# Loading the context already turned, instead of turning it on the chip

## What is computed

```python
def _L0_xattn_ref(key, value, query):
    sim = jnp.einsum('ncs,nds->ncd', key, query) * KC ** (-0.5)   # KC = 128 tokens
    sim = jax.nn.softmax(sim, axis=1)
    context = jnp.einsum('ncd,nds->ncs', sim, value)
    return context
...
x = x + _L0_attn_ref(_layernorm(x, axis=-1), L0_attn_w_q, L0_attn_w_k, L0_attn_w_v, L0_attn_w_o)
x = x + _L0_xattn_ref(ctx_4096, ctx_4096, _layernorm(x, axis=-1))
x = x + _L0_ffn_ref(_layernorm(x, axis=-1), ...)
```

## Time and profile before

| | |
|---|---|
| median of 3 runs | 766.47 us (765.67 to 766.51) |
| the profiled execution | 766.96 us, its span 764.9 us |
| TensorE busy | 740.2 us (97%) |
| VectorE, ScalarE, GpSimd busy | 508.7, 387.0, 309.0 us |
| granted TensorE clock, mean | 0.995 of full |
| moved by DMA | 54.34 MB |

### The profile page before, as it was taken

One profiled execution on the slowest core, in us unless ns is written; L12 is line 12 of the kernel. 1 busy time (PEld: TensorE's weight loads), 2 busy tenths in 40 slices (PEclk: granted clock), 3 DMA queues, 4 the chain that ended last, 5 costly groups with the idle time before them and its releaser, 6 DMA issues.

```text
span 764.9 us, 11284 instructions
## 1 busy us (share of the span) xinstructions
PE 740.2 (97%) x3764; PEld 619.2 (81%) x3764; DVE 508.7 (67%) x669; ACT 387.0 (51%) x969; POOL 309.0 (40%) x334
## 2 busy tenths in 40 slices
PE   7999999999999999999999999999999969999994
PEld 6888888888888888888888888888888747888873
DVE  6457736864675577457836864675447877998897
ACT  3365536443553555265536443553566655656642
POOL 4352314322331432152314322331334543689886
PEclk9999999999999999999999999999999999999998
DMA  9412033212313040213023101303500002212102
GB/s 298 117 57 79 1 106 110 78 41 65 131 57 96 10 168 9 96 57 111 0 86 110 58 33 34 132 5 123 165 1 2 1 0 56 69 55 77 28 10 110
DMA packets 43807, 54.34 MB, mean 71 GB/s; under 512 B 7400, under 2 KB 26024, under 8 KB 43784
## 3 DMA queue, kind: packets, MB, share of 16 engines
q1 hardware_dynamic: 43784, 54.05, 21.9%
HBM read 43.16 MB, written 10.88 MB: 71 GB/s over the span
## 4 chain that ended last, share of the span: by engine, by line
PE 89%; DVE 4%; issue 2%; POOL 2%; ACT 1%; DMA 1%; POOLq 0%; SPq 0%; DVEq 0%; ACTq 0%
PE psum L439 20%; PE psum L441 20%; PE psum L440 20%; PE psum L566 7%; PE psum L628 5%; PE psum L629 5%; PE psum L575 3%; PE psum L650 2%; PE psum L651 2%; PE psum L445 1%; DVE stats L1096 1%; PE psum L459 1%; DMA xacc<-in_x 1%; DVE xacc L1212 1%; PE psum L544 0%
## 5 line engine op out<-in xcount | busy, mean ns | idle before, releaser
L1012 POOL TENSOR_TENSOR probs<-probs,rowinv 128x512 f32<-128x512 f32 x64 | 71.2, 1112 | 308.5 <-DVE rowinv L1241 308.5
L830 ACT ACTIVATE probs<-probs,negmax 128x128 f32<-128x128 f32 x256 | 99.8, 391 | 60.3 <-DVE negmax L1228 60.3
L439 PE MATMUL psum<-xt_hi,wq_hi 128*128 128x512 f32 x256 | 104.4, 408 | 0.0
L439 PE MATMUL psum<-wo_hi,at_hi 128*128 128x512 f32 x256 | 100.2, 391 | 0.5 <-DVE at_lo L1259 0.5
L823 ACT CAST pt_hi<-psum 128x512 fp32r<-128x512 f32 x64 | 37.6, 587 | 124.6 <-PE psum L575 124.6
L441 PE MATMUL psum<-xt_hi,wq_lo 128*128 128x512 f32 x256 | 100.2, 391 | 0.0
L440 PE MATMUL psum<-xt_lo,wq_hi 128*128 128x512 f32 x256 | 99.9, 390 | 0.0
L441 PE MATMUL psum<-wo_hi,at_lo 128*128 128x512 f32 x256 | 99.7, 389 | 0.0
L440 PE MATMUL psum<-wo_lo,at_hi 128*128 128x512 f32 x256 | 99.6, 389 | 0.0
L1259 DVE TENSOR_TENSOR at_lo<-psum,at_hi 128x512 fp32r<-128x512 f32 x64 | 44.1, 689 | 72.8 <-ACT at_hi L859 72.8
L734 ACT ACTIVATE qt<-psum 128x512 f32<-128x512 f32 x64 | 38.1, 595 | 75.7 <-PE psum L441 74.1
(11 more groups left out here) (136 smaller groups left out, 1641.6 us busy)
## 6 DMA issues: line engine op xcount, KB each, us to landing
wq_raw<-in_L_attn_w_q SPq DMA_DIRECT2D x8, 1024.0 KB, 5.4
wo_raw<-in_L_attn_w_o SPq DMA_DIRECT2D x8, 1024.0 KB, 7.7
unpacked_w<-u_q SPq DMA_DIRECT2D x8, 688.0 KB, 3.0
gw<-unpacked_w SPq DMA_DIRECT2D x20, 256.0 KB, 3.5
unpacked_w<-u_q SPq DMA_DIRECT2D x6, 512.0 KB, 2.6
u_q<-in_L_ffn_gate_qweight SPq DMA_DIRECT2D x8, 344.0 KB, 7.3
u_q<-in_L_ffn_up_qweight SPq DMA_DIRECT2D x8, 344.0 KB, 3.8
u_q<-in_L_ffn_down_qweight SPq DMA_DIRECT2D x10, 256.0 KB, 3.3
```

The costliest lines, as they stand in the source:

```text
L439: pe.matmul(dst, a_hi, b_hi, start=start, stop=False)
L830: e = act.activation(probs[:, t % 2, j, :], probs[:, t % 2, j, :], ACT.Exp, bias=negmax[:, t % 2, j:j + 1], accum_out=rowsum[:, t % 2, j:j ...
L1012: pool.tensor_tensor(probs[:, t % 2], probs[:, t % 2], rowinv[:, t % 2, :].unsqueeze(2).to_broadcast([P, HG, P]), ALU.mult).then_inc(prob_ ...
```

## The change

The kernel gets the context a second time as `ctx_turned`, a [512, 1024] array: the same numbers, width first, laid out by the host. SyncE loads it straight into `cxt`, in two halves of 1 MB. The first goes over `wq_raw` and waits until all first-half weights of the last pass are split (`w_lo`). The second goes over the k and v weights and waits until the v projection of the last pass is done. Both stand between the load of `cx` and the first loads of `gw`. `turn_context` on TensorE (32 transposes), `context_first` on ScalarE (8 copies) and their two semaphores are gone. `cross_scores` waits for the two loads, `cross_output` for the load of `cx`; what had waited for the copies to release PSUM bank 5 waits for `proj_out`.

```diff
-    CTX_FILL = {t: (2 * (t - 2), 2 * (t - 2) + 1) for t in range(2, 2 + NB // 2)}
...
+            cxt_v = ctx_turned.rearrange("(c p) t -> p c t", p=P)
+            sp.wait_ge(w_lo, LAST * UNITS + FIRST_UNITS)
+            sp.dma_start(cxt[:, 2:HC], cxt_v[:, 2:HC]).then_inc(ld_cxt, 16)
+            sp.wait_ge(proj_done, LAST * NBLK + FIRST_BLOCKS + BLOCKS.index(("v", 1)) + 1)
+            sp.dma_start(cxt[:, 0:2], cxt_v[:, 0:2]).then_inc(ld_cxt, 16)
...
-            def turn_context(t, k):
-
-                if t in CTX_FILL:
-                    b = CTX_FILL[t][k]
-                    if b == 0:
-                        pe.wait_ge(ld_cx, 16)
-                    elif CTX_BANK[b] == CTX_BANK[b - 1]:
-                        pe.wait_ge(cx_out, b)
-                    else:
-                        pe.wait_ge(proj_out, CTX_BLOCKS)
-                    turn_tile(CTX_BANK[b], cx[:, b, :]).then_inc(cx_turned, 1)
...
-                    pe.wait_ge(cx_out, max(b + 1, CTX_BANK.index(BK_FT)))
+                    pe.wait_ge(ld_cxt, 16 * 2)
...
                     pe.wait_ge(xs_prob, b + 1)
+                    pe.wait_ge(ld_cx, 16)
...
-                        pe.wait_ge(cx_out, NB)
+                        pe.wait_ge(proj_out, CTX_BLOCKS)
...
-                    if not more:
-                        turn_context(t, 0)
...
-                        turn_context(t, 1)
...
-            def context_first(t, k):
-
-                if t in CTX_FILL:
-                    b = CTX_FILL[t][k]
-                    act.wait_ge(cx_turned, b + 1)
-                    act.copy(cxt[:, :, b * P:(b + 1) * P],
-                             psum[:, CTX_BANK[b], :].rearrange("p (c t) -> p c t", c=HC)).then_inc(cx_out, 1)
...
+        if name == "ctx_turned":
+            a = np.asarray(inputs["ctx_4096"])
+            a = a.reshape(-1, a.shape[-1]).T
```

More of the change, by code:

```diff
@@ L23, with decoder_kernel @@
 PRIME = 2
-def decoder_kernel(nc, x, ctx_in, w_q, w_k, w_v, w_o,
+def decoder_kernel(nc, x, ctx_in, ctx_turned, w_q, w_k, w_v, w_o,
                    gate_q, gate_s, gate_z, up_q, up_s, up_z, down_q, down_s, down_z, out):
@@ L124, in decoder_kernel @@
         BK_XT, BK_XS, BK_XC, BK_FT = BK_VT, 7, 3, 5
-        CTX_BANK = [BK_XS] * 4 + [BK_FT] * 4
         unpacked_w = nc.dram_tensor("unpacked_w", [STRIPS, P, INTER], F32)
@@ L182, in decoder_kernel @@
         ld_cx = sem("ld_cx")
+        ld_cxt = sem("ld_cxt")
         consts_pool = sem("consts_pool")
@@ L218, in decoder_kernel @@
         o_added = sem("o_added")
-        cx_turned = sem("cx_turned")
-        cx_out = sem("cx_out")
         xs_done = sem("xs_done")
@@ L838, in group @@
                         v_first(n)
-                    if not more:
-                        context_first(t, 0)
                     for i in FILL[t]:
@@ L865, in group @@
                         queries_out(t)
-                        context_first(t, 1)
                     for unit in SPLIT.get(t, ()):
@@ L1365, in columns @@
     return a.reshape(rows, -1, P).transpose(2, 1, 0)
-_INS = ["x", "ctx_4096", "L0_attn_w_q", "L0_attn_w_k", "L0_attn_w_v", "L0_attn_w_o",
+_INS = ["x", "ctx_4096", "ctx_turned", "L0_attn_w_q", "L0_attn_w_k", "L0_attn_w_v", "L0_attn_w_o",
         "L0_ffn_gate_qweight", "L0_ffn_gate_scales", "L0_ffn_gate_zeros",
@@ L1380 @@
     for name in _INS:
-        a = inputs[name]
+        if name == "ctx_turned":
+            a = np.asarray(inputs["ctx_4096"])
+            a = a.reshape(-1, a.shape[-1]).T
+        else:
+            a = inputs[name]
         if name.endswith("_scales"):
```

## The result

Over 20 runs of each kernel, the changed kernel takes 765.70 us (median, 763.18 to 769.51) and the kernel before 768.48 (765.67 to 770.61). The ratio is 0.9969 [0.9956, 0.9981]: 0.31% faster, or about 2.4 us, with 1.5 to 3.4 us in the interval. A second set of runs, made with the experiments, gives 0.9965 [0.995, 0.998]. The forecast was a gain of 2.20 us, 0.29%. The size of the gain fits the forecast, but the twenty runs leave it open whether it exceeds the 0.2% from which the forecast speaks of faster: the interval begins at 0.19%. The level was not as forecast. The three runs of before that were shown are three of the four lowest among the twenty, and 764.3 was too low by 1.4 us.

A forecast was written before the change was run, and what follows sets the result against it. TensorE was taken as the bound where it runs back to back, other engines' chains elsewhere. Five turns at 0.44 us sum to 2.20 us, taking the 766.47 us median to 764.3 us; range 762.8 to 765.8.

The forecast's parts named there:

- rival 3: A second low-clock stretch of the same size behind 630, giving 765.8 us; chance 0.12.
- (a): TensorE, last pass: one tile's turn is four matmuls and costs 0.44 us; all eight would be 3.5 us.
- (b): Slot t = 2: turns of tiles 0 and 1 are links; everything behind moves by 0.88 us.
- (c): Slot t = 3: tile 2's turn is off the chain, before TensorE's wait for `xn`; worth 0.
- (d): Tiles 3, 4 and 5 are links; the shift reaches 2.20 us at the attention scores of t = 5.
- (e): Tiles 6 and 7: TensorE's further lead is lost because VectorE is the later input at t = 6's mask.
- (g): From t = 6 up to 630.75, every link moves by 2.20 us.
- the low stretch: TensorE at the lower clock from 630.75 to 633.87, price 1.5 us; going away or moving gives 762.8 us, chance 0.08.
- (h): SyncE's loads of `cxt` (9.4 us taken) and the queued `gw` arrive in time; worth 0.
- (f): VectorE's scaling of `xprobs` can't finish while GpSimd multiplies; shift stays 2.20 us, removed ScalarE copies worth 0.
- rivals 4 and 5: 4: waits eat tiles 3 to 5, gain 0.88 us, chance 0.07. 5: lower clock 614 to 630, 769.3 us, 0.04.
- Rival 1: Scaling not held by GpSimd (2.67 us), or VectorE not the later input in t = 6 (3.08); chance 0.12.

The follow-up runs named there:

- the repeat: The changed kernel, unchanged, run and profiled once more: 764.22 us.
- the timed profile: Profile from timing the unchanged changed kernel again beside the kernel before: median 765.33 us, ratio 0.9965.
- experiment 4: Changed kernel with the exponential of the cross scores written to PSUM, where VectorE's scaling of `xprobs` reads it: 763.24 us.
- turns alone: Changed kernel with all eight turns put back on TensorE, results unread, no ScalarE copies: 771.08 us.
- copies alone: Changed kernel with eight spare ScalarE copies put back, no turns: 63.31 us from the last pass's first mask to its last `pt_lo`.
- exponential in PSUM with copies: Changed kernel with the cross-score exponential in PSUM, plus eight spare ScalarE copies: 767.02 us.
- the timed exponential in PSUM: Changed kernel with the cross-score exponential in PSUM, timed beside the kernel before: median 765.10 us, ratio 0.9961.

## Where the prediction failed, and where it held

**The step that failed is the last of the sum: the base.** "The median becomes 764.3" sets the gain of 2.20 on 766.47, the median of three runs. Twenty runs of before have the median 768.48, 2.0 us above it; three runs that agree to 0.8 us were taken for the kernel's level, and the spread of twenty is 5 us. With the right base the same sum gives 766.3, and 765.70 was measured. That 765.70 lies inside the range at all, by 0.1 us, is luck: the upper end, 765.8, was made for a second low stretch (rival 3), not for a base 2 us too low. The step behind it has the same fault. It takes 0.2% (1.5 us) for what a measurement can tell from no change, and gives 0.73 to a gain beyond that. The measured gain is 0.31% with an interval from 0.19% to 0.44%, so a gain is clear and one of more than 0.2% is not. Which of the unsteady terms below lifts the median by 2 us stays open, since the runs without a profile don't show them.

**Each step, by what was measured.** (a) and (b): 0.88 us for tiles 0 and 1, at 0.44 a turn, were forecast; putting them back costs 0.85 to 0.88. (c): tile 2 is worth nothing; the wait for `xn` became 0.81 (0.8 to 0.9 forecast), and 0.40 with tile 2 back. (d): the scores of t = 5 at 574.03 for a forecast 574.0. (e): the mask of t = 6 came without a wait at 583.51 - 0.32 = 583.19 (583.2 forecast), and tiles 6 and 7 are worth nothing. TensorE's scores of t = 6 were forecast near 581 and came at 581.32, since TensorE waits in t = 5 for the bank of the cross output, which VectorE's addition behind the scaling sets free: the wait for VectorE that the prediction announced. (g): 2.17 and 2.19 us reach the end of M. The first gate matmul behind the last wait was forecast at 628.5 or 628.6; it came at 628.34 in the repeat and at 628.36 + 0.22 = 628.58 in the timed profile, but at 629.67 in the first one, where the low stretch moved in front of it. (h): the second load of `cxt` lands 4.9 us after its issue, where 9.4 was taken, and nobody waits.

**(f) was right in what it said and too short in what it covered.** The scalings of slots 4 and 5 take 0.84 and end 0.08 behind GpSimd, as forecast, and experiment 4 shows the hold by taking it away. But "the removed ScalarE copies are therefore worth 0" was looked at in slot 5 alone. In slot 4 a copy stands before `xn`, and once the turns are gone it costs 0.2 us. The sum didn't suffer, since (d) had already moved everything up to 576.19 by all five turns, which is right only with the copies gone. (d) called `query_t` of tile 0 the nearest input that TensorE must find, with 0.5 us to spare. Nearer was `xn` of slot 4, and the rows of before could tell it. It ends at 574.07 and, as part of t = 4, moves by the three turns ahead of that slot's scores, to 572.75. TensorE comes for it at 574.46 less four turns, 572.70. So with the copies in place `xn` would be the later one. Without them it comes half a microsecond sooner: in the changed kernel it ends at 572.62 and TensorE is ready for it at 573.06.

**The unsteady terms were half seen.** The prediction named the low stretch and its price, 1.5 us. The profiles show it moved from 630 to 614 (first profile of the changed kernel), absent until 740 (both profiles of the exponential in PSUM) and doubled (turns alone, copies alone). Moving cost 1.08 us in one piece and gave 1.28 in the next. In the changed kernel it stands at 614 in one profile and behind 626 in two, so there its place belongs to the execution and not to the program; for the other kernels this isn't shown. The first profile of the changed kernel alone shows the signs that the prediction gives for rivals 4 and 5: a gate matmul near 629.9 and a granted clock under 1.00 before 628. Neither rival happened. M is 2.17 shorter in that same profile, where rival 4 has 0.88, and the clock's loss in cross comes back in turn-over. Rival 1 didn't happen either: the scaling takes 0.84 us in slots 4 and 5. What the prediction didn't have are two more unsteady terms, each of the same size: the feed-forward's pace (1.55 us) and a low stretch behind the last addition (0.5 to 1.75 us). Whether transposes hold the clock up the way matmuls do, these runs can't tell: it is 1.00 from 551 to 585 with the turns and without.

A reader of the two first profiles alone would have found equal spans and looked for a loss in the feed-forward that isn't the change's. The repeats of both kernels removed that question.

## What to carry to other kernels

Work taken off a busy engine is worth its slots only up to the next place where another engine's result comes later: here five turns of eight, told in advance by which waits stood behind each. When two pieces of work are removed and each may hide the other, ask for each alone which input comes last once the other is gone, in every slot and not in one. Compare single executions over the stretch that the change touches (here good to 0.03 us), and leave the level to many runs of both kernels, since three runs of one can all lie at one end of its spread.

## What the runs showed of the hardware

**Back-to-back matmuls have two paces at full granted clock.** In the feed-forward, one tile's period between full additions is 10.99 us in nine profiles and 11.20 in four (first profile of the changed kernel, turns alone, exponential in PSUM with copies, the timed exponential in PSUM). It is 0.229 or 0.233 us from matmul to matmul, holds for the whole 101 us, and makes 1.55 us. The changed kernel and the one with the exponential in PSUM each show both. Its cause is open: the granted clock reads 1.00 both ways, and nothing that I changed brings it or takes it away. The median of the twenty runs of before lies 1.5 us above its first profiled execution (766.96), which would fit, but runs without a profile don't show it.

**The low clock behind the feed-forward.** From the last full addition to the end are 24.34 to 24.40 us in seven profiles, and 24.86 to 26.09 in six. Those six have a granted clock under 1.00 (0.72 in the changed kernel's first profile, 0.57 in the exponential in PSUM's) somewhere from 744 to 758 while TensorE still has work; it comes and goes with the program unchanged, as the changed kernel's profiles show.

**VectorE's scaling beside GpSimd**, with its source in SBUF, ends 0.08 us behind GpSimd's multiplication in every slot where they meet, whether it begins 0.28 us after it (0.84 us long), 0.76 (0.36) or 0.80 (0.32); in the last four tiles, where GpSimd's multiplications are over, it takes 0.29 to 0.31. So its row looks short or long by when it began, and the end is what counts.
